# First attention: the denominators of the softmax summed by accumulating DMAs, GpSimd and TensorE

## The reference, cut to what matters

```python
q = _qdq(x) @ _qdq(wq).T + bq
kv = cond @ wkv.T + bkv
k, v = jnp.split(kv, 2, axis=-1)
q = q.reshape(B, N, H, Dh)          # B 4, N 512, H 16 heads, Dh 32
k = k.reshape(B, M, H, Dh)          # M 1601
v = v.reshape(B, M, H, Dh)
scale = 1.0 / np.sqrt(Dh)
attn = jax.nn.softmax(jnp.einsum('bnhd,bmhd->bhnm', q, k) * scale, axis=-1)
o = jnp.einsum('bhnm,bmhd->bnhd', attn, v).reshape(B, N, C)
```

## Time and profile before

| | before |
|---|---|
| median of three runs | 2568.08 us |
| span of the profiled execution | 2568.4 us |
| TensorE busy, whole kernel | 2506.9 us (98%) |
| GpSimd busy, whole kernel | 1286.9 us (50%) |
| additions of the first attention (L1486) | 140 of 4582 ns and 16 of 4575 ns |
| direct sums with ones (L1257) | 288 records, 37.5 us busy |
| a middle unit of the attention | 47.0 us |

### The profile page before, as it was taken

The page is one execution under the profiler, slowest core; times in us unless marked ns, Lnnn a source line. Parts: engine busy times, 40 slices in busy tenths (PEclk is TensorE's granted clock), DMA queues, the critical chain, the costliest instruction groups (busy, mean ns, idle before and its releaser), DMA issues. The chain is left out here.

```text
span 2568.4 us, 33913 instructions
## 1 busy us (share of the span) xinstructions
PE 2506.9 (98%) x13273; PEld 1626.8 (63%) x13288; DVE 1786.5 (70%) x2456; ACT 1223.6 (48%) x1853; POOL 1286.9 (50%) x340
## 2 busy tenths in 40 slices
PE   8999999999999999999998999999999999999998
PEld 8988888987545545555544787788533333335786
DVE  4554554556777767777774676664899999999873
ACT  4222313311666666666664232322688888886110
POOL 0000000000999999999993000000599999997310
PEclk9999999999999999999999999999999999999999
DMA  8677776655535345354323754443997777776300
GB/s 303 212 255 236 265 283 240 221 172 160 115 83 121 68 96 108 68 111 93 68 71 137 246 185 156 155 164 87 245 213 168 167 159 167 159 170 196 120 33 33
DMA packets 218865, 405.10 MB, mean 158 GB/s; under 512 B 18217, under 2 KB 94537, under 8 KB 218641
## 3 DMA queue, kind: packets, MB, share of 16 engines
q1 hardware_dynamic: 218704, 402.93, 56.8%
HBM read 260.63 MB, written 140.59 MB: 156 GB/s over the span
## 5 line engine op out<-in xcount | busy, mean ns | idle before, releaser
L1486 POOL TENSOR_TENSOR pooled<-pooled,probs 128x2048 f32<-128x2048 f32 x140 | 641.5, 4582 | 21.0 <-POOL pooled L1486 0.9
L1345 ACT ACTIVATE probs<-psum 128x512 f32<-128x512 f32 (+1 forms) x832 | 449.6, 600 | 333.6 <-PE psum L1231 328.4
L1372 DVE TENSOR_REDUCE win_max<-psum 128x1 f32<-128x802 f32 x480 | 454.3, 988 | 133.9 <-PE psum L1196 133.6
L2271 DVE TENSOR_SCALAR probs<-psum,bound 128x1024 f32<-128x1024 f32 (+1 forms) x416 | 499.0, 1275 | 31.5 <-POOL pooled L2303 21.3
L2246 ACT ACTIVATE probs<-probs 128x1024 f32<-128x1024 f32 (+1 forms) x416 | 437.6, 1059 | 82.5 <-DVE probs L2271 40.6
L2303 POOL TENSOR_TENSOR pooled<-pooled,probs 128x2048 f32<-128x2048 f32 x92 | 424.2, 4611 | 13.2 <-ACT probs L2246 1.0
L1231 PE MATMUL psum<-q_st,k_st 128*128 128x512 f32 (+1 forms) x832 | 318.7, 436 | 22.2 <-ACT probs L1345 15.6
L312 POOL TENSOR_TENSOR r_q<-ve_q,minus_half 128x4 f32<-128x4 f32 x8 | 9.1, 1133 | 611.3 <-DVE ve_q L256 611.3
L1196 PE MATMUL psum<-k_st,q_st 96*128 96x402 f32 x960 | 265.8, 358 | 0.9 <-DVE o_sb L1391 0.4
L1231 PEld LDWEIGHTS psum<-q_st,k_st 128*128 128x128 f32 (+1 forms) x832 | 149.4, 185 | 180.4 <-ACT probs L1345 130.6
L2214 PE MATMUL psum<-q_st,k_st 128*128 128x512 f32 (+1 forms) x832 | 251.6, 428 | 10.7 <-DVE probs L2271 9.6
(11 more groups left out here) (276 smaller groups left out, 4211.1 us busy)
## 6 DMA issues: line engine op xcount, KB each, us to landing
k_st<-k_hi SPq DMA_DIRECT2D x64, 801.0 KB, 10.6
k_st<-k_lo SPq DMA_DIRECT2D x48, 801.0 KB, 11.1
k_hi<-kt_hi SPq DMA_DIRECT2D x32, 801.0 KB
k_lo<-kt_lo SPq DMA_DIRECT2D x32, 801.0 KB
v_rows<-v_out SPq DMA_DIRECT2D x96, 256.0 KB
v_st<-v_rows SPq DMA_DIRECT2D x24, 768.0 KB
q_st<-q_hi SPq DMA_DIRECT2D x64, 256.0 KB, 8.4
w<-w_hi_d SPq DMA_DIRECT2D x64, 256.0 KB, 3.1
```

The lines of the kernel that those rows point to most:

```text
L1345: A.activation(probs[i % NPROBS][0:rows, j, :], bank(score_banks.where["score", u, t, j])[0:rows, :], ACT.Exp, scale=1.0 / ROOT).then_inc( ...
L1372: V.tensor_reduce(win_max[:, r, j, c:c + 1], window(windows.where["max", u, i])[:, :, 0:MV], AX.XY, ALU.max).then_inc(max_done, 1)
L1486: G.tensor_tensor(pooled[u % 2][:], before[:], probs[tile(u, k) % NPROBS][:], ALU.add).then_inc(pool_added, 1)
L2271: V.tensor_scalar(probs[i % NPROBS][0:rows, half * W:half * W + W, :], window(("score", u, t, half))[0:rows], bound[0:rows, u // NG, t:t + 1],
```

## The change

Now all 13 tiles of a unit are pooled (8 in the last unit). Tile 2p + 1 is added into tile 2p by an accumulating DMA that GpSimd issues (`add_pair`), six such pairs in a unit. GpSimd adds pair 0 and pair 1 into `pooled`, then the other pairs, and the odd tile 12 (`add_lone`): six additions. The direct sums of the tiles 11 and 12 are gone, and `last_sum` stands alone in step 5 (`SUM_AT`) of the next unit, so only the steps 5 and 6 have two score banks. The last unit still sums five tiles (8 to 12) directly. There are nine buffers of probabilities and one `pooled` in place of eight and two. The closing of the units 13 and 14 moves from step 4 to 6, the rows of the last unit from step 5 to 7.

```diff
-            NQ, NSLOT, NPROBS, LAG, TURN_AT, WINDOWS = 3, 3, 8, 2, 11, 3
-            LAST_SUM, CODES_AT, ROWS_AT = 1, 3, 5
+            NQ, NSLOT, NPROBS, LAG, TURN_AT, WINDOWS = 3, 3, 9, 2, 11, 3
+            SUM_AT, CODES_AT, ROWS_AT = 5, 3, 7
...
-                pooled = [sbuf(f"pooled0{i}", [P, HPG, S]) for i in range(2)]
+                pooled = sbuf("pooled0", [P, HPG, S])
...
                 def three_banks(u, t):
-                    return 5 <= t < pooled_tiles(u) + LAG
+                    return t not in (SUM_AT, SUM_AT + 1) and t < pooled_tiles(u) + LAG
...
+                def pairs(u):
+
+                    return TT // 2 if u < UNITS - 1 else 4
+
                 def pooled_tiles(u):
-
-                    return 11 if u < UNITS - 1 else 7
+                    return TT if u < UNITS - 1 else 2 * pairs(u)
+
+                def pair(u, p):
+                    d = u * (TT // 2) + p
+                    return pair_added[d % 2], 16 * (d // 2 + 1)
...
                     def last_sum(u):
-                        M.wait_ge(pool_added, adds(u + 1))
+                        alone = pooled_tiles(u) == TT
+                        if alone:
+                            take_den(u)
+                        if u == 0:
+                            M.wait_ge(set_up, 1)
+                        M.wait_ge(pool_added, sum_ready(u))
                         for j in range(HPG):
-                            m = M.matmul(den[j * DH:(j + 1) * DH, :], ones[:], pooled[u % 2][:, j, :], start=False, stop=True)
+                            m = M.matmul(den[j * DH:(j + 1) * DH, :], ones[:], pooled[:, j, :], start=alone, stop=True)
...
                             pu, pt = divmod(i - NPROBS, TT)
                             if pt < pooled_tiles(pu):
-                                A.wait_ge(pool_added, pool_reads(pu, pt))
+                                if pt == TT - 1:
+                                    A.wait_ge(pool_added, lone_added(pu))
+                                elif pt % 2:
+                                    A.wait_ge(*pair(pu, pt // 2))
+                                else:
+                                    A.wait_ge(pool_added, added(pu, pt // 2))
...
                 def pool_program():
+                    def add_pair(u, p):
+
+                        d = u * (TT // 2) + p
+                        G.wait_ge(exp_done, score(u, 2 * p + 1, HPG))
+                        G.wait_ge(tile_read, tile(u, 2 * p) + 1)
+                        if d >= 2:
+                            G.wait_ge(pair_added[d % 2], 16 * (d // 2))
+                        G.dma_start(flat(of(u, 2 * p)), flat(of(u, 2 * p + 1)),
+                                    accum_op=ALU.add).then_inc(pair_added[d % 2], 16)
+
+                    def add(u, p):
+                        if p == 1:
+                            if u:
+                                G.wait_ge(summed, u)
+                            G.wait_ge(*pair(u, 0))
+                            before = of(u, 0)
+                        else:
+                            G.wait_ge(pool_added, added(u, p) - 1)
+                            before = pooled
+                        G.wait_ge(*pair(u, p))
+                        G.tensor_tensor(pooled[:], before[:], of(u, 2 * p)[:], ALU.add).then_inc(pool_added, 1)
...
                     for u in range(UNITS):
-                        for k in range(1, pooled_tiles(u)):
...
+                        if u:
+                            add_lone(u - 1)
+                            add(u - 1, pairs(u - 1) - 1)
+                        add_pair(u, 0)
+                        add_pair(u, 1)
+                        for p in range(1, pairs(u) - 1):
+                            add_pair(u, p + 1)
+                            add(u, p)
+                    add(UNITS - 1, pairs(UNITS - 1) - 1)
```

More of the change, by code:

```diff
@@ L1233, in scores, with take_den @@
                         score_banks.freed_by(exp_done, score(u, t, j) + 1)
+                    def take_den(u):
+                        _, free = score_banks.take(("sum", u), among=(7,))
+                        M.wait_ge(*free)
+                        score_banks.freed_by(den_copied, u + 1)
                     def values(u, t):
@@ L1310, in pe_program @@
                             values(*behind)
-                            if behind[1] == LAST_SUM and behind[0]:
-                                last_sum(behind[0] - 1)
+                        if now and now[0] and now[1] == SUM_AT:
+                            last_sum(now[0] - 1)
                         if now:
@@ L1349, in copy_acc @@
                     def copy_acc(u):
-                        A.wait_ge(accumulated, u + 1)
+                        A.wait_ge(tile_read, tile(u + 1, 0))
                         if u:
@@ L1363, in act_program @@
                             copy_acc(behind[0])
-                        if behind and behind[1] == LAST_SUM and behind[0]:
-                            copy_den(behind[0] - 1)
+                        if now and now[0] and now[1] == SUM_AT:
+                            copy_den(now[0] - 1)
                     copy_den(UNITS - 1)
@@ L1475, in pool_program, with of @@
                 def pool_program():
-                    for u in range(UNITS):
-                        for k in range(1, pooled_tiles(u)):
-                            G.wait_ge(exp_done, score(u, k, HPG))
-                            if k == 1:
-                                if u >= 2:
-                                    G.wait_ge(summed, u - 1)
-                                before = probs[tile(u, 0) % NPROBS]
-                            else:
-                                G.wait_ge(pool_added, adds(u) + k - 1)
-                                before = pooled[u % 2]
-                            G.tensor_tensor(pooled[u % 2][:], before[:], probs[tile(u, k) % NPROBS][:],
-                                            ALU.add).then_inc(pool_added, 1)
+                    def of(u, t):
+                        return probs[tile(u, t) % NPROBS]
@@ new lines, in add_lone @@
+                    def add_lone(u):
+                        rows = TROWS[TT - 1]
+                        G.wait_ge(exp_done, score(u, TT - 1, HPG))
+                        G.wait_ge(pool_added, lone_added(u) - 1)
+                        G.tensor_tensor(pooled[0:rows, :, :], pooled[0:rows, :, :], of(u, TT - 1)[0:rows, :, :],
+                                        ALU.add).then_inc(pool_added, 1)
+                    for u in range(UNITS):
+                        if u:
[6 more added lines that the diff above has]
+                            add(u, p)
@@ L1531, in sp_program @@
                             if u + 1 < UNITS:
-                                Y.wait_ge(accumulated, u)
+                                Y.wait_ge(tile_read, tile(u, 0))
                                 load_v(u + 1)
```

27 lines of the change are left out of this document (14 added, 13 removed).

## The result

The kernel after takes 2632.52 us (median; 2628.9 to 2636.51), the kernel before on the same chip 2567.82 (2567.28 to 2570.58). The ratio is 1.0251, with a 95% interval of 1.0236 to 1.0265: 2.5% slower, 102 us above the forecast of 2530 and above the range. The profiled execution has a span of 2627.1 us.

A forecast was written before the change was run, and what follows sets the result against it. TensorE was taken to set the pace, with GpSimd full too: 34.3 us gained in units 1 to 14 plus 4.1 in the last make 38.4, and 2568.4 - 38.4 = 2530 us. Range 2522 to 2625 us, the forecast's own 2522 to 2541.

The forecast's parts named there:

- the order of banks: Steps 2, 4 and 6 of a unit: two gain 0.23 us each with three score banks, step 6 loses 0.23.
- The issue: GpSimd's issue of each accumulating transfer: 0.5 us taken, 3.5 kept for the range, up to 2.0 us allowed.
- Rival D: On GpSimd: an issue costs more than 2 us; at 3.5 us the kernel takes 2596 us; chance 0.05.
- one pass: Accumulating transfer of 1 MB: 2.4 us moving plus 2.1 fixed, 4.5 us to landing; two passes would be 6.9.
- half the engines' time: Pairs 0 and 1 share the DMA engines with the loads, landing 9 to 12 us after issue.
- the limit: Pairs 0 and 1 must land some 12 us after their issue, by 27 us into the unit.
- B: Rival: pairs 0 and 1 land 1 to 4 us late, ScalarE or TensorE waits; 2541 to 2586 us; chance 0.25.
- one us per us late: Price of pairs 0 and 1 landing later than 12 us after issue: each us adds a us per unit.
- C: Rival: DMA engines become the bound, two-pass transfers and loads adding up to 49.8 us per unit; 2603 to 2640; chance 0.22.
- C's sign: In the trace after: a DMA share near 1 through the whole unit and a unit above 47 us.
- E: Rival: another limit behind, VectorE's maxima, keeps steps long; half the gain above the floor goes; 2541 to 2560; chance 0.06.
- Unit 0 stays as it is: First unit of the attention: no direct sum in its early steps, so no change in its time.

The follow-up runs named there:

- tiny: The kernel after with each accumulating transfer cut to 64 of its 2048 columns, all waits, issues and additions kept: 2536.32 us, ratio 0.9879.
- nosums: The kernel before without the direct sums of tiles 11 and 12 (tile 7 in the last unit), GpSimd's additions left as they were: 2567.27 us, ratio 0.9998.
- copy: The kernel after with plain copies in place of the accumulating transfers, same tiles and bytes, still issued by GpSimd: 2541.91 us, ratio 0.9901.
- bufs8: The kernel after with eight buffers of probabilities instead of nine: 2679.49 us, ratio 1.0433.
- copy01: The kernel after with plain copies for pairs 0 and 1 alone, the other four pairs accumulating: 2584.32 us, ratio 1.0063.
- copy34: The kernel after with plain copies for pairs 3 and 4 alone, the other pairs accumulating: 2621.74 us, ratio 1.0208.
- early0: The kernel after with GpSimd issuing pair 0 before the addition of pair 5 of the unit before: 2594.57 us, ratio 1.0102.
- mix4: Against the kernel after: tiles 0 to 3 added singly by GpSimd, four accumulating pairs from tile 4 on, eight buffers, two pooled tiles: 2543.46 us, ratio 0.9906.
- cutloads: The kernel after with two thirds of the loads of keys and queries cut to 64 columns from unit 3 on: 2560.80 us, ratio 0.9971.

## Where the prediction was right, and where it failed

**The bound and the gain (right in kind, a little large).** TensorE set the pace, a direct sum costs what was read, and the unit that waits for nothing is 44.9 us, forecast 44.6. By the same starts, four steps of a unit fall by 1.10, 1.09, 0.90 and 0.24 us, and three around the moved sum rise by 0.44, 0.24 and 0.54, where 0.23 in all had been set for the order of banks. So a unit gains 2.1 us and not 2.45, and the last unit 2.1 (3.0 in tiny) and not 4.1. The run tiny, the same schedule with its transfers made light, ends at 2536 against 2530.

**GpSimd is right behind TensorE (half said).** The prediction read that GpSimd could take no more, but put the whole gain down to TensorE's sums. nosums shows that taking them away alone gives nothing: the relief of GpSimd, and so the transfers, are needed for the first microsecond of the gain.

**The issue (right).** 0.87 us on GpSimd where 0.5 was taken and 3.5 kept as a bound; 32.4 us of work in a unit. Rival D is out.

**The time of a transfer (the step that failed).** Two choices were made in one paragraph, and both were wrong.
First, one pass. This one decided. The text had both ends, 4.5 and 6.9 us to landing, and took the lower. The shortest of 94 transfers took 6.9, and engine time is 5.14 us against 2.81 for a copy of the same bytes. The Trainium skill (Collectives: The Full Stack, The bandwidth ceiling: the fold count and why AG ≠ RS ≠ AR) says that an add inside the DMA engine needs two reads and runs at half the rate of a copy; 0.63 against 0.32 us for a packet of 8 KB agrees.
Second, "half the engines' time". The loads reach half the best rate, and the text took that as room for a second stream. The trace after shows none: with loads queued in front, pairs 0 and 1 moved nothing until 21.2 us into the unit. 5.4 us of waiting and the 6.9 of the shortest landing put pair 0 at 12.3 us, and the rest of the loads in between makes 13.8 on average in units 3 to 12; pair 1, behind it, took 17.5. 9 to 12 was forecast, and 12 was the limit. With one pass the same standing still stays inside the limit (11.6 and 11.4 us in copy), so in a middle unit this second choice costs nothing without the first.

**The rivals.** The mechanism is B's, to the step: ScalarE waits in step 9 for pairs 0 and 1, and nearly only there (unit 1, behind the first loads, loses 4 us in step 5 and 2 in step 9). The price "one us per us late" was about right. In units 3 to 12 ScalarE starts step 9 at 38.2 us of the unit, 5.9 later than in tiny, and the unit is 6.2 longer, 4.5 of it TensorE standing still and 1.7 the lower clock; in bufs8 it is 9.7 longer for 8.8 us late. B ended at 2586 because it took 1 to 4 us of lateness. The size is C's: 2632 is in its 2603 to 2640, and C's sign, an engines' share of 0.99, is there too. Its premise held: loads and transfers add up, 31 and 20 us of engine time in a unit of 51. But it isn't what holds the unit. Had throughput been the only bound, bufs8 would not be 47 us slower, copy01 and copy34 would be alike, and early0 could not move the same bytes 2 us per unit faster. The engines' limit stands close behind all the same: they are busy 98% of a unit of early0, and how far below its 48.7 us they would allow with all loads and six accumulating transfers, no run tells. By luck both rivals' effects give about the same length of unit, so C's number alone would have looked like a proof of C.

Three numbers of the rivals don't follow from their own terms: B's lower end is 2530 + 14 = 2544 and not 2541, C's upper one is 2645 and not 2640, and half of E's gain above the floor is 6 us, 2536. None of them changes the range.

**Unit 0 (missed).** "Unit 0 stays as it is" cost 6.7 us. It was judged by its direct sums, of which it has none early, and not by the transfers, of which it gets six, amid the first loads. It is 43.1 us in tiny and 43.7 in mix4, 48.4 in copy and 49.6 in the kernel after.

**The range.** It ended at 2625, with C's upper part left out. The numbers at hand would have carried B past its 2586: loads that fill the engines until 20 us into the unit, then two transfers of 4.8 and 2.1 fixed, are 31.7 against the 27 that is wanted, so 4.7 us for each of 14 units, 2596. B's price had to be worked out with the longer transfer and no sharing, as C's was. The rest is of sizes: 14 units at 6.1 us instead of 4.7 (85 in all), 5 and 2 us less gain in these and in the last one, and 6.7 in unit 0. Together with 2530 that is 2629, for a measured span of 2627.1.

Open: in which order the engines serve the two queues. It isn't strict order of issue over all that is queued (in early0 both moved side by side), nor packet by packet in turn from the start (the kernel after). Mending unit 1 of mix4, some 6 us, was tried once, without success.

## What to carry to other kernels

A transfer that takes work off a full engine isn't free because it is asynchronous: ask when it is issued, what is queued in front of it at that moment, and when its buffer is wanted, and price it with the longer of two durations as long as no row decides. A reuse distance in buffers is time: one buffer is one step of 3.4 us here, and lateness beyond it is paid in full, part of it as TensorE's lower clock. If some of the moved work falls into a stretch in which the DMA engines are full, leave that part where it was (mix4), before you look for another way to move all of it.

## What the runs showed of the hardware that was not expected

- An accumulating transfer of 1 MB from SBUF to SBUF holds the 16 engines for 5.14 us and lands 6.9 us after its issue at best; a plain one holds them for 2.81, and its median to landing was 6.3 us (copy). GpSimd's issue takes 0.87 us for the one and 0.58 for the other.
- Transfers of two queues delayed each other. Two issued behind loads moved nothing for 6 us (the kernel after, and the same with plain copies), and loads issued behind a transfer moved 0.03 MB in 4.8 us.
- With a stop of about 4.5 us in each unit, TensorE's clock was at 1.2 GHz for 3.4 to 6.8 us per unit: 1.7 us more for every such stop.
- A DMA share of 0.95 to 0.97 was seen in units that waited for nothing (cutloads, unit 14 of the kernel after), and of 0.89 in units of 51 us in which TensorE stood still for about 4 us (copy34). The share did not tell whether transfers held the kernel up.
- In mix4 a VectorE operation on 128x4 elements, 0.26 us in the kernel after, took 4.32 us, from 1346.57 on. It began 0.25 us after an addition on GpSimd and ended with it:
```profile
1346.57 4.32 DVE L256 TENSOR_SCALAR ve_first<-mv_first 128x4 f32<-128x4 f32 x1
```
```profile
1346.32 4.55 POOL L1527 TENSOR_TENSOR pooled<-pooled,probs 128x2048 f32<-128x2048 f32 x1 [2.18 <-DMA probs<-probs]
```
